# An attention output projected group by group with 128x128 products, its bias added on GpSimd, and other slot orders

## What is computed

```python
x = x + 0.5 * ffn(layernorm(x))     # 16 experts of 64, top 4 by groups, and one shared expert of 128
x = x + attention(layernorm(x))
x = x + 0.5 * ffn(layernorm(x))

# attention: 16 query heads of 8, one key and one value head, window of 32 to each side
probs = softmax(where(|i - j| <= 32, q k^T / sqrt(8), -1e30))
out   = (probs v).reshape(b, t, 128) @ Wf.T + bf
```

## Time and profile before

| | us |
|---|---|
| median of 3 runs | 331.09 (330.57 to 335.35) |
| the profiled execution, its own time | 330.3 |
| its span | 328.5 |

### The profile page before, as it was taken

The page is one execution under the profiler, slowest core; times in us unless marked ns, Lnnn a source line. Parts: engine busy times, 40 slices in busy tenths (PEclk is TensorE's granted clock), DMA queues, the critical chain, the costliest instruction groups (busy, mean ns, idle before and its releaser), DMA issues.

```text
span 328.5 us, 4752 instructions
## 1 busy us (share of the span) xinstructions
PE 277.2 (84%) x1404; PEld 181.9 (55%) x1404; DVE 186.0 (57%) x583; ACT 150.3 (46%) x285; POOL 139.7 (43%) x167
## 2 busy tenths in 40 slices
PE   0768759999989996688886898595988999999995
PEld 0646327666656654354563474263865766766662
DVE  1586432848982467559466558642366485494230
ACT  3556134456432225546546746565263544632220
POOL 4710377155743597145134142400233816652740
PEclk9989969999999999979999899999799999999999
DMA  6300907255956833644865732103500801703511
GB/s 180 111 0 5 308 17 266 71 134 142 245 137 215 209 64 106 159 73 147 157 99 151 154 68 56 39 19 77 185 1 4 257 0 52 239 3 105 187 32 32
DMA packets 44355, 37.00 MB, mean 113 GB/s; under 512 B 18888, under 2 KB 32810, under 8 KB 44330
## 3 DMA queue, kind: packets, MB, share of 16 engines
q1 hardware_dynamic: 43306, 36.44, 41.5%
q0 software_dynamic: 1024, 0.26, 0.4%
HBM read 31.76 MB, written 4.84 MB: 111 GB/s over the span
## 4 chain that ended last, share of the span: by engine, by line
PE 56%; DVE 17%; issue 10%; ACT 8%; DMA 4%; POOL 2%; SPq 1%; DVEq 0%; ACTq 0%; POOLq 0%
PE pY L957 14%; PE pY L1043 4%; PE pU L1030 4%; PE pG L875 3%; DVE ring L740 3%; PE pG L876 3%; PE pG L877 3%; PE pU L876 3%; PE pU L877 3%; PE pU L875 3%; PE pG L1015 3%; PE p L1085 3%; DMA X<-x 2%; DVE neg_max L777 2%; SPq L281 1%
## 5 line engine op out<-in xcount | busy, mean ns | idle before, releaser
L459 POOL TENSOR_TENSOR ring<-ring,c_all 128x512 f32<-128x512 f32 x64 | 80.7, 1280 | 74.6 <-DMA c_all<-comb_dram 40.0
L740 DVE TENSOR_TENSOR ring<-ring,pU 128x512 f32<-128x512 f32 x72 | 49.2, 684 | 60.6 <-PE pU L877 41.0
L535 ACT ACTIVATE ring<-pG 128x512 f32<-128x512 f32 x72 | 42.6, 597 | 80.1 <-PE pG L877 76.0
L957 PE MATMUL pY<-ring,wd_sb 128*128 128x512 f32 x144 | 74.7, 612 | 2.8 <-POOL ring L459 2.7
L875 PE MATMUL pG<-xt_hi,wg_hi 128*128 128x512 f32 x72 | 53.3, 740 | 2.0 <-ACT ring L535 1.9
L571 ACT ACTIVATE probs<-pU 128x512 f32<-128x512 f32 x64 | 34.6, 595 | 9.6 <-PE pU L1030 9.4
L777 DVE TENSOR_REDUCE neg_max<-pG 128x8 f32<-128x768 f32 x32 | 30.5, 952 | 10.2 <-PE pG L1015 9.9
L957 PEld LDWEIGHTS pY<-ring,wd_sb 128*128 128x128 f32 x144 | 25.8, 193 | 13.3 <-issue 5.8
L875 PE MATMUL pU<-xt_hi,wu_hi 128*128 128x512 f32 x72 | 29.2, 406 | 2.4 <-DVE ring L740 2.4
L1015 PE MATMUL pG<-k_diag,q_rep 128*128 128x384 f32 x64 | 21.1, 411 | 9.8 <-issue 5.1
L876 PE MATMUL pG<-xt_hi,wg_lo 128*128 128x512 f32 x72 | 29.2, 406 | 0.0
(11 more groups left out here) (137 smaller groups left out, 425.1 us busy)
## 6 DMA issues: line engine op xcount, KB each, us to landing
c_all<-comb_dram SPq DMA_DIRECT2D x64, 256.0 KB, 4.3
q_stage<-q_dram SPq DMA_DIRECT2D x16, 192.0 KB
q_t<-q_dram SPq DMA_DIRECT2D x16, 192.0 KB
k_diag<-k_dram SPq DMA_DIRECT2D x32, 72.0 KB
q_dram<-q_hi SPq DMA_DIRECT2D x8, 256.0 KB, 3.0
q_t<-qrows_dram SPq DMA_DIRECT2D x2, 576.0 KB
X<-x SPq DMA_DIRECT2D x4, 256.0 KB, 3.9
q_dram<-q_lo SPq DMA_DIRECT2D x4, 256.0 KB, 3.0
```

The costliest lines, as they stand in the source:

```text
L459: pool.tensor_tensor(ring[:, n % RING], ring[:, n % RING], c_all[:, n % CH], ALU.mult)\
L535: act.activation(ring[:, n % RING], pG[:, n % 2], ACT.Silu).then_inc(silu_done, 1)
L740: dve.tensor_tensor(ring[:, n % RING], ring[:, n % RING], pU[:, n % 2], ALU.mult).then_inc(gu_done, 1)
L957: pe.matmul(pY[:, u % 2], wd_sb[:, D * e:D * (e + 1)], ring[:, n % RING], start=e == 0, stop=e == CH - 1)\
```

## The change

The 16 products and the bias product of a batch become one 128x128x128 fp32 product per group. For this, ACT's copy of the weighted values (`copy_o`) reorders the columns while it copies, and the host orders `Wf` to match. `project(n)` now writes the second quarter of bank p1, in slot n + 5; DVE adds 128x128 per group. The bias is a 128x512 addition on POOL, once a batch (`add_bias`, at FFN1 33 and attention slots 1, 5, 9). `output_to_columns` waits for the addition of the group before. The orders change too: POOL issues `max_rows` ahead of `normalize_attention`; ACT does `copy_o` behind all four `exps`; PE puts the second half of `scores` between two halves of `weighted_values`; DVE does both kinds of layernorm and the route steps at the end of an attention slot; the steps of FFN2's first batch behind `layernorm(4)` move one slot up; the last slots interleave FFN2 0, 1, 2 with attention 18, 19, 20.

```diff
 def timeline():
-    for t in range(NG + 3):
+    for t in range(NG + 2):
         order.append((ATTN, t))
         order += late[2 * t:2 * t + 2]
-    order += [(FFN2, 0), (ATTN, NG + 3)]
-    order += [(FFN2, s) for s in range(1, SLOTS)]
+    for t in range(3):
+        order += [(FFN2, t), (ATTN, NG + 2 + t)]
+    order += [(FFN2, s) for s in range(3, SLOTS)]
...
-X_NORM = {... (ATTN, 11): 4, ...}     X_COLUMNS = {... (ATTN, 12): 4, ...}     LOGITS = {... (ATTN, 13): 4, ...}
+X_NORM = {... (ATTN, 10): 4, ...}     X_COLUMNS = {... (ATTN, 11): 4, ...}     LOGITS = {... (ATTN, 12): 4, ...}
-         (ATTN, 14): (4, 0, 7), (ATTN, 15): (4, 7, 14), (ATTN, 16): (4, 14, 21)}
+         (ATTN, 13): (4, 0, 7), (ATTN, 14): (4, 7, 14), (ATTN, 15): (4, 14, 21)}
-COMB = {... (ATTN, 17): 4, ...}
+COMB = {... (ATTN, 16): 4, ...}
-PROJECT = {(ATTN, 7): 0, (ATTN, 11): 1, (ATTN, 15): 2, (ATTN, 19): 3}
+BIAS = {(FFN1, 33): 0, (ATTN, 1): 1, (ATTN, 5): 2, (ATTN, 9): 3}
...
+            def add_bias(a):
+                pool.wait_ge(axn_done, a + 1)
+                pool.wait_ge(attn_w_in, 4 * 16)
+                pool.tensor_tensor(X[:, a], X[:, a], bias_sb[:].unsqueeze(1).to_broadcast([P, NT, D]), ALU.add)\
+                    .then_inc(bias_added, 1)
...
                 for n in chunks(kind, t, HID_LAG):
                     if n % CH < NP2:
                         hid(n)
+                if kind == ATTN and 1 <= t <= NG:
+                    max_rows(t - 1)
                 if slot in XA_NORM:
                     normalize_attention(XA_NORM[slot])
-                if kind == ATTN and 1 <= t <= NG:
-                    max_rows(t - 1)
+                if slot in BIAS:
+                    add_bias(BIAS[slot])
                 if slot in Q_SPREAD:
                     spread_q(*Q_SPREAD[slot])
...
             def copy_o(n):
-                act.activation(o_raw[:], pY[:, 0], ACT.Copy).then_inc(o_copied, 1)
+                act.activation(o_raw[:].rearrange("p (h b q) -> p b h q", b=2, q=64),
+                               pY[:, 0].rearrange("p (b h q) -> p b h q", b=2, q=64), ACT.Copy).then_inc(o_copied, 1)
...
-                if kind == ATTN and 0 <= t - 3 < NG:
-                    copy_o(t - 3)
                 if kind == ATTN and 0 <= t - 2 < NG:
                     exps(t - 2, 2)
                     exps(t - 2, 3)
+                if kind == ATTN and 0 <= t - 3 < NG:
+                    copy_o(t - 3)
...
-            def add_attention(a):
-                slab = X[:, a].rearrange("p t d -> p (t d)")
-                dve.wait_ge(attn_psum, a + 1)
-                dve.tensor_tensor(slab, p0[:], slab, ALU.add).then_inc(attn_added, 1)
+            def add_attention(n):
+                a, g = divmod(n, G4)
+                dve.wait_ge(attn_psum, n + 1)
+                dve.wait_ge(bias_added, a + 1)
+                dve.tensor_tensor(X[:, a, g], p1[:, P:2 * P], X[:, a, g], ALU.add).then_inc(attn_added, 1)
...
+                if kind == ATTN:
+                    if slot in X_STATS:
+                        layernorm(X_STATS[slot])
+                    if slot in XA_STATS:
+                        attention_layernorm(XA_STATS[slot])
+                    if slot in ROUTE:
+                        r, lo, hi = ROUTE[slot]
+                        for k in range(lo + 1, hi + 1):
+                            route(r, k)
...
-                pe.matmul(p0[:].rearrange("p (t d) -> p t d", d=D), ones_rows[:],
-                          bias_parts[:].unsqueeze(1).to_broadcast([BR, NT, D]), start=True, stop=False)
-                for g in range(G4):
-                    for i in range(2):
-                        for b in range(2):
-                            rows = slice(64 * b, 64 * (b + 1))
-                            ins = pe.matmul(p0[rows, P * g:P * (g + 1)], o_t[rows, g, 64 * i:64 * (i + 1)],
-                                            wf_sb[rows, i], start=False, stop=g == G4 - 1 and i == 1)
-                ins.then_inc(attn_psum, 1)
+            def project(n):
+                pe.wait_ge(ot_copied, n + 1)
+                pe.matmul(p1[:, P:2 * P], o_t[:, n % NQ], wf_sb[:], start=True, stop=True).then_inc(attn_psum, 1)
...
                     key_scores(t - 2, 0)
                     key_scores(t - 2, 1)
+                if kind == ATTN and 0 <= t - 5 < NG:
+                    project(t - 5)
                 if kind == ATTN and 0 <= t - 4 < NG:
                     output_to_rows(t - 4)
+                if kind == ATTN and 0 <= t - 3 < NG:
+                    weighted_values(t - 3, 0)
                 if kind == ATTN and t < NG:
                     scores(t, 1)
                 if kind == ATTN and 0 <= t - 3 < NG:
-                    weighted_values(t - 3)
+                    weighted_values(t - 3, 1)
```

More of the change, by code:

```diff
@@ L36 @@
 PARTS = 3 * HD
+NQ = 4
 KQ = 98
@@ L62 @@
 X_STATS = {(FFN1, 0): 1, (FFN1, 7): 2, (FFN1, 16): 3, (ATTN, 9): 4, (ATTN, 14): 5, (FFN2, 7): 6, (FFN2, 16): 7}
-X_NORM = {(FFN1, 2): 1, (FFN1, 9): 2, (FFN1, 18): 3, (ATTN, 11): 4, (ATTN, 16): 5, (FFN2, 9): 6, (FFN2, 18): 7}
-X_COLUMNS = {(FFN1, 3): 1, (FFN1, 10): 2, (FFN1, 19): 3, (ATTN, 12): 4, (FFN2, 1): 5, (FFN2, 10): 6, (FFN2, 19): 7}
-LOGITS = {(FFN1, 4): 1, (FFN1, 11): 2, (FFN1, 20): 3, (ATTN, 13): 4, (FFN2, 2): 5, (FFN2, 11): 6, (FFN2, 20): 7}
+X_NORM = {(FFN1, 2): 1, (FFN1, 9): 2, (FFN1, 18): 3, (ATTN, 10): 4, (ATTN, 16): 5, (FFN2, 9): 6, (FFN2, 18): 7}
+X_COLUMNS = {(FFN1, 3): 1, (FFN1, 10): 2, (FFN1, 19): 3, (ATTN, 11): 4, (FFN2, 1): 5, (FFN2, 10): 6, (FFN2, 19): 7}
+LOGITS = {(FFN1, 4): 1, (FFN1, 11): 2, (FFN1, 20): 3, (ATTN, 12): 4, (FFN2, 2): 5, (FFN2, 11): 6, (FFN2, 20): 7}
 ROUTE_STEPS = 21
@@ L74 @@
             ROUTE[(_kind, _s + _i)] = (_r, _a, _b)
-COMB = {(FFN1, 4): 0, (FFN1, 9): 1, (FFN1, 17): 2, (FFN1, 26): 3, (ATTN, 17): 4, (FFN2, 8): 5, (FFN2, 17): 6,
+COMB = {(FFN1, 4): 0, (FFN1, 9): 1, (FFN1, 17): 2, (FFN1, 26): 3, (ATTN, 16): 4, (FFN2, 8): 5, (FFN2, 17): 6,
         (FFN2, 26): 7}
@@ L529, in combine_columns @@
                 wait(act, comb_stored, 16 * r)
-                act.activation(comb_t[:], p1[0:E, :], ACT.Copy).then_inc(comb_t_done, 1)
+                act.activation(comb_t[:], (p0 if r == NB else p1)[0:E, :], ACT.Copy).then_inc(comb_t_done, 1)
             def silu(n):
@@ L824, in _ @@
                 kind, t = slot
-                if slot in ROUTE:
+                if slot in ROUTE and kind != ATTN:
                     r, lo, hi = ROUTE[slot]
@@ L836, in _ @@
                     negated_max(t, 0)
-                if slot in X_STATS:
+                if slot in X_STATS and kind != ATTN:
                     layernorm(X_STATS[slot])
@@ L844, in _ @@
                     attention_weights_lo()
-                if slot in XA_STATS:
+                if slot in XA_STATS and kind != ATTN:
                     attention_layernorm(XA_STATS[slot])
@@ L912, in combine_to_columns @@
                 for t in range(NT):
-                    ins = pe.transpose(p1[0:32, P * t:P * (t + 1)], comb[:, t], ident[:])
+                    ins = pe.transpose((p0 if r == NB else p1)[0:32, P * t:P * (t + 1)], comb[:, t], ident[:])
                 ins.then_inc(comb_psum, 1)
@@ L1031, in key_scores, with weighted_values @@
                           start=True, stop=True).then_inc(st_psum, 1)
-            def weighted_values(n):
+            def weighted_values(n, b):
                 a, g = divmod(n, G4)
-                pe.wait_ge(exp_done, 4 * n + 4)
-                wait(pe, o_copied, n)
-                if n == 0:
-                    pe.wait_ge(y_copied, 3)
-                if g == 0:
-                    pe.wait_ge(v_done, a + 1)
-                for b in range(2):
-                    for j in range(4):
-                        ins = pe.matmul(pY[32 * j:32 * j + 32, 0, 256 * b:256 * (b + 1)], v_one[:, a % 2, 2 * g + b],
-                                        probs[:, n % 2, 2 * b + j // 2, 256 * (j % 2):256 * (j % 2 + 1)],
-                                        start=True, stop=True)
-                ins.then_inc(pv_psum, 1)
+                if b == 0:
+                    pe.wait_ge(exp_done, 4 * n + 4)
+                    wait(pe, o_copied, n)
+                    if n == 0:
+                        pe.wait_ge(y_copied, 3)
+                    if g == 0:
+                        pe.wait_ge(v_done, a + 1)
+                for j in range(4):
+                    ins = pe.matmul(pY[32 * j:32 * j + 32, 0, 256 * b:256 * (b + 1)], v_one[:, a % 2, 2 * g + b],
+                                    probs[:, n % 2, 2 * b + j // 2, 256 * (j % 2):256 * (j % 2 + 1)],
+                                    start=True, stop=True)
+                if b == 1:
+                    ins.then_inc(pv_psum, 1)
             def output_to_rows(n):
@@ L1134, in _ @@
                     v_to_rows(V_ROWS[slot])
-                if slot in PROJECT:
-                    project(PROJECT[slot])
             pe.wait_ge(logits_done, UNITS)
```

69 lines of the change are left out of this document (20 added, 49 removed).

## The result

The changed kernel takes 339.8 us in the median of four runs (336.6 to 345.2), the kernel before beside it 332.2 (330.6 to 335.4). The ratio is 1.020, with a 95% interval of 1.012 to 1.028: slower, by about 2%. The profiled execution took 336.6 us with a span of 334.7, against 330.3 and 328.5 before. What an edit does is read from landmarks of the profiles.

The account below looks back on a forecast made before the run. PE was taken to fill the last 90.2 us; no engine is full in the attention part, where PE's idle gaps count. +7.0 + 0.4 - 3.9 = +3.5 on 330.3 gave 333.8, median 334.6 us, range 327.5 to 340.

Parts of the forecast that it names:

- Slot 10: Attention slot 10: statistics behind k_lo delay POOL's row transfers; key_scores(8) at 188.1 instead of 178.54, +9.5 us.
- (a): Rival, slot 10: row transfers land in 2 us also under load, opening it 3.0 us sooner; 331.6 us, chance 0.15.
- Slot 8: Attention slot 8: starts 0.2 us earlier, about 5 us of PE idle time ahead, and costs 1.5 us more.
- Slots 12 to 17: Attention: slot 12 is 7.0 us later, slot 16 still +7.0, slots 16 and 17 together add +0.4.
- The project: Projection on PE: 16 products of 0.25 us, 4.0 us in place of 9.6.
- The tail: From output_to_columns(13) to FFN2 3: 12.7 us instead of 16.6, -3.9 (bounds -5 and -2.5).
- The bias: POOL's 4 x 1.04 us; in FFN1 33 it delays PE's down ahead of slot 1 by about 0.6 us.
- Slot 4: Attention slot 4: with the attention statistics moved, it starts 0.6 us earlier (0 to 1.2) against the bias.
- Slot 15: Attention slot 15: the same move of statistics makes key_scores(13) +1.9 us later, with a wait of about 5 us.
- (b): Rival, slots 10 and 15: loads hold the row transfers as long as ever seen, +1.8 each; 338.2 us, chance 0.20.
- (c): Rival, slot 10: moving the statistics costs nothing, slot 12 +0.8 instead of +7.0; 328.4 or 326.5 us, chance 0.17.
- (d): Rival, whole edit: only hidden work moves, the projection's time goes to the batch entries; 331 us, chance 0.05.

Follow-up runs that it names:

- e3: Changed kernel, but SP holds back batch 3's k_diag and q_stage loads in slot 10 until group 8's row transfers have landed; ratio to before 1.018.
- e10: e9 with the preparation of batches 2 and 3 one slot earlier; ratio to the kernel before 0.987.
- e11: e10 with only SP's queue reordered: next batch's stores and the q_t and k_t loads go earlier; median 319.1 us, ratio to before 0.958.
- e2: Changed kernel with POOL doing max_rows ahead of rstd_of in slots 9 and 14; ratio to the kernel before 1.002.
- e9: e5 with e2's edit, max_rows ahead of rstd_of on POOL; ratio to the kernel before 0.989.
- e6: e5 with the last slots in the old order too; median 334.5 us, ratio to the kernel before 1.001.
- e7: Changed kernel without the bias additions on POOL and DVE's wait for them; span of the one execution 338.8 us.
- e1: Changed kernel with FFN2's statistics, layernorm(4) and layernorm(5), back ahead of q_lo and k_lo on DVE; median 334.5 us, no ratio.
- e5: Changed kernel with old orders inside attention slots: both layernorms ahead on DVE, copy_o before the last exps, weighted_values whole; median 330.6 us, ratio to before 0.981.

## Why the prediction was right, and where not

The sum said 333.8 us for the profiled execution and 334.6 for the median, slower than before by 1%, mainly by the wait in slot 10. Measured were 336.6 and 339.8; the range (327.5 to 340.0) holds them, the latter barely. A loss of 3.5 us was forecast, and 6.3 came by the profiled executions, 7.6 by the medians.

*Slot 10.* The decisive step held nearly to the number: `mv` behind `k_lo`, `rstd_of` ahead of `max_rows`. POOL could issue at 182.2 (182.5 was said), PE resumed at 187.5 (188.1), slot 12 began at 198.3 (198.3). That the last agrees to the tenth is luck: PE resumed 0.6 us early, and from there to slot 12 it took 10.8 us instead of 10.2. The landing was taken as 5.0 us and was 3.6 to 4.4; e3 shows that the loads beside it are the cause of what exceeds 2 us, and so rival (a) falls. The Trainium skill ("DMA: Bandwidth & Descriptors", Queues, rings and completion order) has each DMA engine take turns between queues; the trace shows that turns don't spare a small transfer a doubled landing time, 1.8 to 2.4 us alone and 3.6 to 4.4 beside the loads.

*Slot 8.* Its start was right (165.5 against 166.4), but not the way there. I put 5 us of idle time on PE ahead of slot 8 and a low clock in it. In fact there was no gap. PE waited 2.30 us in slot 6, and the clock fell in slot 7, which took 6.45 us at 0.56:

```profile
153.92 0.85 DVE L665 BATCH_NORM_STATS2 astats<-X 128x6 f32<-128x128 f32 x4
...
156.08 0.62 PE L1028 MATMUL pG<-k_diag,q_rep 128*128 128x384 f32 x2 [2.30 <-DVE neg_max L782]
...
159.04:165.49 6.45, 6.45 (x32) 3.92 (x32) 3.31 (x9) 1.59 (x5) 2.19 (x3) 0.56 0.70 148
165.49:170.69 5.20, 4.61 (x37) 2.90 (x36) 3.67 (x9) 3.27 (x8) 2.15 (x3) 1.00 0.47 103
```

The attention statistics, moved to the end of slot 5, stood ahead of the next slot's `neg_max`. My account asked what they no longer delay, and not what they delay now. The transfer chain hid that mistake: POOL's copy of `q_stage` ended at 165.35, so slot 8 couldn't have begun sooner. That chain was mis-sized too, 11.5 us from `k_lo` to the scores instead of 13. The 1.5 us that I added to slot 8 for a fallen clock came as well (5.20 against 3.82), but at a clock of 1.00; that is luck.

*Slots 12 to 17, the step that failed.* For these slots the sum has single projects and nothing for ACT's order or for the split on PE; I had ACT's order only in slots 5 and 9. It put POOL's issue of `max_rows(13)` 16.7 us behind the start of slot 12 (208.0 less 191.3 in the old count), and it came 18.7 behind:

```profile
216.95 2.23 POOL L472 DMA_DIRECT2D q_t<-max_t  x4 [0.61 <-issue]
```

So from slot 12 to key 13 it was 21.3 us, not 19.3, and from key 13 to rows 13 it was 13.5, not 11.5. Together 4.0 us; less what the tail and the last stretch did better (0.7 and 0.5 us) that is the excess of the span over the forecast (334.7 against 332.0). Runs with the old orders show what the new ones cost where no statistics stand and the clock is full: slot 12 takes 4.88 us in the changed kernel and 4.5 in e10 and e11, slot 13 takes 4.88 and 4.2, and from key 13 to rows 13, with no wait for row transfers, e2 (new orders) takes 13.9 and e9, e10 and e11 (old orders) 12.9. That is 2.1 of the 4.0 us. The rest isn't parted: slot 14, which has the statistics in one order and not in the other, POOL's `rstd` to issue (2.2 us instead of 1.9), and the clock in slot 15, 0.73 behind the wait of 6.1 us. The loop that I read from the timeline (second pair of `key_scores`, two exponentials, `copy_o`, `o_t`, then `project` in the next slot, 4.88 us round) fits these numbers, but it is argued from the rows and not tested by itself.

*The project.* 0.25 us a piece was estimated; the distance to the next start is 0.22 to 0.33 at full clock and 0.42 at low clock. That its move off the batch's end is a gain isn't shown: e6, with it and the old orders and tail, is level with the kernel before.

*The tail.* 12.7 us said, 12.0 measured, of 16.6 before.

*The bias.* 0.6 us said for slot 0, 0 to 0.66 by e3 and e7. A pass was taken at 1.04 us and took 1.27 to 1.29.

*Slot 4.* 0.6 us earlier was said; it started at 141.2 against 141.1.

*Slot 15.* A wait of about 5 us was said and 6.1 came.

*The rivals.* (b) is not what happened, although the size of the loss fits it: the landings were short, the slots long. (c) is refuted by the wait of 10.6 us, which fell to 2.0 when e1 put the statistics back; its price of 7 us was too high for e1's profiled execution, where slot 12 came 4 to 6 us sooner and the fallen clock took 3 back. (d) is refuted for the whole edit, which is 2% slower. For the product and the bias alone e6 bears it out: level with before, and the projection's time stands as a wait ahead of slot 8.

## What to carry to other kernels

When an instruction moves to the end of a slot, follow the queue of every engine that waits for it: an unmoved waiter (`rstd_of`) that stands ahead of an urgent issue (`max_rows`) turns a move of a microsecond on DVE into 8 us on PE. A wait that is taken away gives only what lies between it and the next late thing: e2 removed 16.7 us of waits and won some 6, and e9 and e10 each removed the waits they aimed at and were no faster beyond the noise than the run they were built on (ratios 0.981, 0.989, 0.987), until e11 also had the transfers in the right order. Splitting a block or swapping two copies can lengthen every slot of a pipeline, so such small reorderings belong in the sum with the number of slots as a factor.

## What the runs showed of the hardware that I had not expected

A gap on PE can cost more than its own length. Behind the gap of 4.1 us in e1, slot 12 ran at a granted clock of 0.57 and took 7.9 us; the same slot took 4.9 us at 1.00 in the changed kernel. With the old orders it is the same: 7.3 us at 0.58 in e9, behind a wait of 4.9, and 4.5 us at 1.00 in e10. Not every gap does this: behind the wait of 2.74 us in slot 15 before, the clock stayed at 1.00 up to rows 13. The mean clock of the attention part was 0.96 before, 0.89 changed, 0.90 in e5 and 0.97 in e11, and the ranking of the last three is that of their times, which by itself doesn't say which causes which. The clock can also fall a slot late: behind 2.30 us in slot 6 it was low in slot 7, and full again in slot 8.

Small transfers of 8 KB landed in 1.8 to 2.4 us when SP held its loads back and in 3.6 to 4.4 us beside them, with nothing else changed in the program. The Trainium skill ("DMA: Bandwidth & Descriptors", Latency and other measured facts) gives an HBM access 0.2 us on average and 2 us under high load; that would be of this size, but no run here tells the memory's part from the engines' queues.
